# A fused Mamba and mixture-of-experts kernel on one core: the expert part moved to earlier slots, u and delta*u in one buffer

## The reference, cut to what matters

```python
x = x + layernorm(mamba(layernorm(x)))      # the first residual is called x1 here
x = x + layernorm(moe(layernorm(x)))

# mamba, D_INNER = 512, 16 states, 4 taps
x_in, z = split(x @ W_in)
u = silu(conv(x_in) + conv_b)
dt, B, C = split(u @ W_xproj)
delta = softplus(dt @ W_dt + b_dt)
h[t] = exp(delta[t] * A) * h[t-1] + (delta[t] * u[t]) * B[t]     # for each of 16 states n
y[t] = sum over n of h[t] * C[t] + D_skip * u[t]
out = (y * silu(z)) @ W_out

# moe: 2 shared and 8 routed experts of width 128
coef = top-2 of softmax(x @ router)
out = sum over e of (silu(x @ gate_e) * (x @ up_e)) @ down_e, times coef_e for the routed ones
```

## Time and profile before

| what | value |
|---|---|
| median of three runs | 2786.3 us |
| the profiled execution's own time | 2785.2 us |
| its span in the profile | 2783.4 us |
| first scan | 70.81 us |
| one body in the middle (scan of slot 0 to the next) | 166.50 us |
| end of the last scans to the end of the span | about 100 us |

### The profile page before, as it was taken

How to read it: one execution, slowest core, us unless ns; L and a number is a source line. 1 busy time by engine, 2 the same in 40 slices (tenths; PEclk the granted TensorE clock), 3 DMA queues, 4 the chain that set the end, 5 groups by cost and what they waited for, 6 DMA issues and landing times. The chain is left out here.

```text
span 2783.4 us, 31976 instructions
## 1 busy us (share of the span) xinstructions
PE 2355.8 (85%) x9920; PEld 1493.7 (54%) x9920; DVE 2325.4 (84%) x3308; ACT 1844.2 (66%) x2632; POOL 1789.7 (64%) x1470
## 2 busy tenths in 40 slices
PE   6678988889798888988889798898988889797878
PEld 3345655556455555655556455555655556455554
DVE  2899888888889888888888889888888888889970
ACT  3555857768586685857768576685857768586652
POOL 2465775847668485675847668485775847658653
PEclk9758989999898998989999898998989999899899
DMA  3101111111111111121112111111111112111111
GB/s 109 34 32 43 49 58 35 54 39 57 50 43 46 48 49 49 47 60 35 53 39 57 49 43 47 43 54 50 46 61 35 53 39 58 38 43 52 52 42 38
DMA packets 92954, 134.38 MB, mean 48 GB/s; under 512 B 12000, under 2 KB 42976, under 8 KB 92784
## 3 DMA queue, kind: packets, MB, share of 16 engines
q1 hardware_dynamic: 92784, 132.34, 16.2%
HBM read 123.13 MB, written 9.18 MB: 48 GB/s over the span
## 5 line engine op out<-in xcount | busy, mean ns | idle before, releaser
L760 DVE TENSOR_TENSOR_SCAN h<-d_a,carry,d_bu 128x512 f32<-128x512 f32 x1024 | 1306.1, 1276 | 118.5 <-ACT d_a L596 112.0
L1000 POOL TENSOR_TENSOR d_bu<-delta_u,b_rows 128x1024 f32<-128x1024 f32 x512 | 1199.3, 2358 | 4.4 <-issue 0.2
L596 ACT ACTIVATE d_a<-delta,a_neg 128x512 f32<-128x512 f32 x1024 | 701.9, 689 | 608.3 <-DVE h L760 602.3
L448 PE MATMUL ht<-ident,h 128*128 128x128 f32 x4096 | 677.7, 295 | 184.4 <-DVE y_t L777 156.0
L448 PEld LDWEIGHTS ht<-ident,h 128*128 128x128 f32 x4096 | 525.0, 151 | 570.8 <-issue 284.6
L777 DVE SCALAR_TENSOR_TENSOR y_t<-ht,c_t,y_t 128x512 f32<-128x512 f32 x896 | 658.8, 735 | 126.4 <-PE ht L448 125.2
L1042 POOL TENSOR_TENSOR hidden<-silu_gate,up 128x512 f32<-128x512 f32 x160 | 203.9, 1274 | 346.5 <-issue 284.9
L530 PE MATMUL dn<-w_down_sb,hidden 128*128 128x256 f32 x1280 | 331.3, 405 | 90.6 <-POOL hidden L1047 69.8
L503 PE MATMUL ring<-x_t,w_gate_sb 128*128 128x512 f32 x640 | 328.7, 639 | 19.8 <-ACT delta L716 16.7
L530 PEld LDWEIGHTS dn<-w_down_sb,hidden 128*128 128x128 f32 x1280 | 247.0, 203 | 132.3 <-POOL hidden L1047 73.7
L510 PE MATMUL ring<-x_t,w_up_sb 128*128 128x512 f32 x640 | 303.8, 597 | 0.0
(11 more groups left out here) (114 smaller groups left out, 2410.3 us busy)
## 6 DMA issues: line engine op xcount, KB each, us to landing
b_rows<-b_rows_hbm SPq DMA_DIRECT2D x256, 256.0 KB, 3.5
coef_rows<-coef_rows_hbm SPq DMA_DIRECT2D x128, 256.0 KB, 3.5
xa<-L_attn_x_in SPq DMA_DIRECT2D x16, 512.0 KB, 5.0
xr<-L_attn_x_in SPq DMA_DIRECT2D x16, 512.0 KB, 3.8
out<-xr SPq DMA_DIRECT2D x16, 512.0 KB, 3.1
w_in_sb<-L_attn_W_in_in SPq DMA_DIRECT2D x1, 1024.0 KB, 6.4
w_gate_sb<-L_ffn_experts_gate_in SPq DMA_DIRECT2D x2, 512.0 KB, 5.0
w_up_sb<-L_ffn_experts_up_in SPq DMA_DIRECT2D x2, 512.0 KB, 5.7
```

Source lines behind the costliest of these rows:

```text
L448: last = nc.tensor.transpose(HT[q % HTS][:, j * P:(j + 1) * P], H[:, (NS * c + n) % HS, j, a * P:(a + 1) * P], IDN[:, :])
L596: nc.scalar.activation(DA[i % DAS][:, :], DL[:, r, j, :], ACT.Exp, scale=ANEG[:, j, n:n + 1]).then_inc(ex.sem, 1)
L760: nc.vector.tensor_tensor_scan(H[:, (NS * s + n) % HS, j, :], DA[(n * J + j) % DAS][:, :], BU[:, (2 * n + j // 2) % 4, j % 2, :], CARRY[:, ...
L1000: nc.gpsimd.tensor_tensor(BU[:, (2 * n + h) % 4, :, :], DU[:, 2 * h:2 * h + 2, :], BB[:, n % 2, :].unsqueeze(1).to_broadcast([P, 2, T]), A ...
```

## The change

The slots are set anew. The transposes, gates and output products of the former chunk stand closer together and earlier, the transposes of x1 go to the two `DN` banks and not through the ring, router and first gate product share slot 19, each expert keeps four slots, and its down product stands five slots behind its gate product, not six. So the last down product is in slot 60 of its own body, the moments of the result in slots 62 and 63, and its residual in slot 1 of the next. D_skip*u (`DU`) now comes before delta (`DL`). U has two buffers in turn, and delta*u is written over u, on GpSimd in slots 44, 45, 48 and 49. The core of the diff:

```diff
-        U = sb("u", [P, J, T])
+        U = sb("u", [P, 2, J, T])
         YD = sb("y_d", [P, J, T])
         SZ = sb("silu_z", [P, 2, NT, DI])
         DL = sb("delta", [P, 2, J, T])
-        DU = sb("delta_u", [P, J, T])
...
-        XIN_PE, TAP0_ACT = (2, 3, 9, 11), (3, 4, 10, 12)
-        TAP = ((4, 4, 4), (5, 5, 5), (11, 11, 12), (13, 13, 14))
-        YD_PE, YD_ACT, OUT_PE = (5, 6, 7, 8), (6, 7, 8, 9), 10
-        Z_PE = (13, 15, 18, 19)
-        SILU = {10: [("u", 0), ("u", 1)], 16: [("u", 2), ("u", 3), ("z", 0), ("z", 1)], 20: [("z", 2), ("z", 3)]}
-        XD_PE, X1T_PE, ROUTE_PE, GATE_PE, CT_PE, CF_PE = 17, 22, 24, 24, 27, 31
-        DL_PE, DL_ACT = (35, 35, 39, 39), (36, 36, 40, 40)
-        DU_PE, DU_ACT = (43, 43, 47, 47), (44, 44, 48, 48)
+        XIN_PE, TAP0_ACT = (5, 6, 9, 10), (6, 7, 10, 11)
+        TAP = ((7, 7, 8), (8, 9, 9), (11, 11, 11), (12, 12, 13))
+        YD_PE, YD_ACT, OUT_PE = (3, 3, 4, 4), (4, 4, 5, 5), 6
+        Z_PE = (12, 14, 17, 18)
+        SILU = {11: [("u", 0), ("u", 1)], 15: [("u", 2), ("u", 3), ("z", 0), ("z", 1)], 19: [("z", 2), ("z", 3)]}
+        X1T_PE, GATE_PE = 18, 19
+        XD_PE, CF_PE, CT_PE = 21, 25, 26
+        DU_PE, DU_ACT = (29, 30, 33, 34), (30, 31, 34, 35)
+        DL_PE, DL_ACT = (37, 37, 41, 41), (38, 38, 42, 42)
+        DU_POOL = (44, 45, 48, 49)
...
+        def silu_slot(f):
+            return GATE_PE + 4 * f + 1
...
-            return gate_slot(f) + 6
-
-        MIDDLE = {0: [("ct", 1, 0)], 1: [("cf", -1, 0)], 2: [("dl", 1, 0), ("dl", 1, 1)],
-                  3: [("dl", 1, 2), ("dl", 1, 3)], 4: [("du", 1, 0), ("du", 1, 1)],
-                  5: [("du", 1, 2), ("du", 1, 3)]}
-        RING_USE = [("xt", 1, 0, 0), ("xt", 1, 1, 1), ("xin", 1, 0, 0), ("xin", 1, 1, 1)]
+            return gate_slot(f) + 5
+
+        MIDDLE = {0: [("xd", 1, 0, 0)], 1: [("cf", -1, 0, 0), ("ct", 1, 0, 1)],
+                  2: [("du", 1, 0, 0), ("du", 1, 1, 1)], 3: [("du", 1, 2, 0), ("du", 1, 3, 1)],
+                  4: [("dl", 1, 0, 0), ("dl", 1, 1, 1)], 5: [("dl", 1, 2, 0), ("dl", 1, 3, 1)]}
+        RING_USE = [("xt", 1, 0, 0), ("xt", 1, 1, 1)]
         RING_USE += [("yd", -1, j, j % 2) for j in range(J)]
-        RING_USE += [("xin", 1, 2, 0), ("xin", 1, 3, 1), ("z", 1, 0, 0), ("z", 1, 1, 1), ("xd", 1, 0, 0),
-                     ("z", 1, 2, 1), ("z", 1, 3, 0), ("x1t", -1, 0, 0), ("x1t", -1, 1, 1)]
-        experts = [use for k in range(F) for use in [("gt", -1, k), ("up", -1, k)] + MIDDLE.get(k, [])]
-        RING_USE += [(*use, i % 2) for i, use in enumerate(experts)]
-
-        ring_free = {"yd": (yd, 1), "xt": (xt, 1), "xin": (conv, TAPS), "z": (sz, 1), "x1t": (x1t, 1),
+        RING_USE += [("xin", 1, j, j % 2) for j in range(J)] + [("z", 1, a, a % 2) for a in range(NT)]
+        for k in range(F):
+            RING_USE += [("gt", -1, k, 0), ("up", -1, k, 1)] + MIDDLE.get(k, [])
...
-                    if exists(lo - 2) and t == 10:
+                    if exists(lo - 2) and t == 3:
...
-                    if ffn and t == 12:
+                    if ffn and t == 4:
...
-                    if ffn and t < NT:
-                        transpose_state(s - 1, t - NT + SLOTS)
-                    if exists(lo - 2) and t == 1:
-                        down_part(s - 2, F - 1)
...
-                    if ffn and t in (20, 21, 23, 26):
-                        if t == 20:
-                            pe.wait_ge(resid["o"].sem, resid["o"].at(s - 1))
-                        keep_warm(DN[1])
+                    if ffn and t == 2:
+                        pe.wait_ge(*ring_user_before(s, lo, "yd", 0))
+                        keep_warm(ring_bank("yd", 0))
+                        keep_warm(ring_bank("yd", 0))
                     if ffn and t == OUT_PE - 1:
                         pe.wait_ge(resid["y"].sem, resid["y"].at(s - 2, 2))
                         keep_warm(DN[0])
                         keep_warm(DN[0])
+                    if ffn and t in (15, 16):
+                        if t == 15:
+                            pe.wait_ge(resid["o"].sem, resid["o"].at(s - 1))
+                        keep_warm(DN[1])
...
-                        pe.wait_ge(*ring_user_before(s, lo, "x1t", k))
-                        bank = ring_bank("x1t", k)
                         for a in range(NT):
-                            last = nc.tensor.transpose(bank[:, a * P:(a + 1) * P],
+                            last = nc.tensor.transpose(DN[k][:, a * P:(a + 1) * P],
...
-                if t == ROUTE_PE:
+                if t == GATE_PE:
...
-                    if exists(lo - 2) and t == 9:
+                    if exists(lo - 2) and t == 2:
...
-                        act.wait_ge(full["xd"].sem, full["xd"].at(c - 1))
-                        act.wait_ge(full["du"].sem, full["du"].at(c - 1))
-                        act.wait_ge(du.sem, du.at(c - 1))
-                        nc.scalar.activation(U[:, j, TAPS - 1:], ring_bank("xin", j)[:, TAPS - 1:], ACT.Identity,
+                        act.wait_ge(bu.sem, bu.at(c - 2))
...
-                    if ffn and t <= NT:
-                        add_state(s - 1, o, SLOTS + t - NT - 1)
-                        if t > 0:
-                            gate_y(s - 1, o, t - 1)
+                    if ffn and t == 0:
+                        add_state(s - 1, o, SLOTS - NT - 1)
+                    if ffn and t in (1, 2):
+                        for a in (2 * t - 2, 2 * t - 1):
+                            add_state(s - 1, o, SLOTS - NT + a)
+                            gate_y(s - 1, o, a)
...
-                if t in (3, 4):
-                    dve.wait_ge(down.sem, down.at(c))
-                    for a in (2 * t - 6, 2 * t - 5):
-                        moments("y", c, a, dn(a))
-                if t == 4:
-                    moments_end("y", c)
-                if t in (7, 8):
-                    for a in (2 * t - 14, 2 * t - 13):
+                if t == 1:
+                    for a in range(NT):
...
-                if t in (OUT_PE + 2, OUT_PE + 5):
-                    a = 0 if t == OUT_PE + 2 else 2
+                if t in (8, 11):
+                    a = 0 if t == 8 else 2
...
-                if t in (17, 18):
-                    for a in (2 * t - 34, 2 * t - 33):
+                if t in (13, 14):
+                    for a in (2 * t - 26, 2 * t - 25):
                         add_stream_o(c, a)
-                if t == 19:
+                if t == 15:
...
-                if t == ROUTE_PE + 1:
+                if t == GATE_PE + 1:
                     route(c, 0)
                     route(c, 1)
-                if ROUTE_PE + 3 <= t < ROUTE_PE + 7:
-                    for i in range(4):
-                        route(c, 4 * (t - ROUTE_PE - 3) + 2 + i)
-            def conv_part(c, t):
+                if t in (GATE_PE + 3, GATE_PE + 4):
+                    for i in range(8):
+                        route(c, 8 * (t - GATE_PE - 3) + 2 + i)
+                if t in (62, 63):
+                    dve.wait_ge(down.sem, down.at(c))
+                    for a in (2 * t - 124, 2 * t - 123):
+                        moments("y", c, a, dn(a))
+                    if t == 63:
+                        moments_end("y", c)
...
-                    if exists(lo - 2) and t == 5:
-                        rstd_of("y", s - 2)
-                    if ffn and t == OUT_PE + 5:
+                    if ffn and t == 63:
+                        rstd_of("y", s - 1)
+                    if ffn and t == 11:
                         rstd_of("o", s - 1)
-                    if ffn and t == 20:
+                    if ffn and t == 16:
...
+                for j in range(J):
+                    if t == DU_POOL[j]:
+                        pool.wait_ge(softplus.sem, softplus.at(c, j + 1))
+                        pool.wait_ge(full["xd"].sem, full["xd"].at(c))
+                        pool.wait_ge(full["du"].sem, full["du"].at(c))
+                        nc.gpsimd.tensor_tensor(U[:, o, j, :], DL[:, o, j, :], U[:, o, j, :], ALU.mult)\
+                          .then_inc(du.sem, 1)
...
-                    for j in (t - 60, t - 59):
-                        pool.wait_ge(softplus.sem, softplus.at(c, j + 1))
-                        pool.wait_ge(u_s.sem, u_s.at(c))
-                        if j == 0:
-                            pool.wait_ge(bu.sem, bu.at(s))
-                        nc.gpsimd.tensor_tensor(DU[:, j, :], DL[:, o, j, :], U[:, j, :], ALU.mult)\
-                          .then_inc(du.sem, 1)
```

More of the change, by code:

```diff
@@ L358, in body @@
                           .then_inc(xr_ld.sem, 16)
-                    if ffn and t in (33, 34):
-                        coef_row(s - 1, 1 - r, t - 33)
-                    if ffn and t > 34 and t % 4 == 1 and 2 <= (t - 29) // 4 < E:
-                        coef_row(s - 1, 1 - r, (t - 29) // 4)
-                    if prep and t == 22:
+                    if ffn and t in (CF_PE + 2, CF_PE + 3):
```

(31 more changed lines are left out.)

9 lines of the change are left out of this document (6 added, 3 removed).

## The result

The changed kernel takes 2855.6 us (2852.95 to 2856.72) where the kernel before takes 2786.7 beside it: a ratio of 1.025 [1.0237, 1.0262], slower by 69 us. The profiled execution has a span of 2854.6 us, 71.2 more than before. VectorE works 9 us less in total than in the earlier trace rows and waits more.

The account below looks back on a forecast made before the run. What can change is VectorE's waiting, about 20 us a chunk, since neither TensorE nor VectorE is simply the limit. Fourteen chunks at +5.0 (+70) and the tail (+16) give 86 on 2785.2, taken as 2872; range 2765 to 2925.

Parts of the forecast that it names:

- Slots 0 to 12, 42.1: Front of the chunk: two new VectorE waits, 5.7 us, replace 3.5 and a tap moves in; 38.94 becomes 42.1, +3.2.
- Slots 12 to 28, 44.4: Stretch with all routing: VectorE's waits 5.1 against 7.4, including 3.4 for the router; 46.86 becomes 44.4, -2.5.
- Slots 28 to 44, 35.9: Stretch that loses the routing operations, -2.7, its other waits at about the same price; 39.05 becomes 35.9, -3.15.
- Slots 44 to 64, 17.85 and 31.25: Deciding term: GpSimd late for the eighth expert's down product, VectorE waits 6.1; 16.90 becomes 17.85, 24.75 becomes 31.25.
- The sum, +5.0 for each of fourteen chunks: The stretches add up to 171.5 us a chunk, +5.0; fourteen chunks have all three parts: +70.
- Lead-in and body 0 at nothing: Lead-in within 1 us, y_init before delta with the same products; first chunk, without experts, nothing, -3 to +3.
- Body 15 at nothing: The chunk without preparation, so no delta*u on GpSimd: no change, -3 to +3 us.
- The tail, +16: Last chunk's experts: each from the second on takes 7.05 us, not 5.16; seven times 1.9 plus 2.9 at the start.
- Edits at nothing: Two u buffers, delta*u in place, earlier result store, moved b_store and coef_row, two more warmers a chunk: no cost.
- A: Rival, slots 0 to 5: low clock lengthens the queue to the second output product by 4 us, 2928 total; chance 0.14.
- B: Rival: one of two TensorE waits (GpSimd's 6.1 or the front's 5.7) is absorbed, tail stays, 2785 to 2815; chance 0.22.
- C: Rival: neither TensorE wait reaches VectorE, -6.8 us a chunk, faster kernel at 2706; chance 0.18.

Follow-up runs that it names:

- n1: The changed kernel with every expert's down product six slots behind its gate, as before, instead of five: 2786.8 us, 1.0003 of the kernel before.
- k4: The changed kernel with three warming products ahead of the eighth expert's down product, where TensorE waits for hidden: 2840.9 us, 1.0202 of the kernel before.
- k3: The changed kernel with the down product six slots behind its gate in the last chunk's experts alone: 2831.5 us, 1.017 of the kernel before.
- n5: The changed kernel without the two warming products of slot 5, ahead of the output products: 2825.5 us, 1.0146 of the kernel before.
- k1: The changed kernel with distance six, delta*u four slots earlier, first moments of o in slot 9, routing one slot later, no slot-5 warmers: 2717.3 us, 0.9753 of before.
- m1: The changed kernel with down products six slots behind the gate and delta*u in slots 40, 41, 44, 45: 2785.0 us, 1.0 of the kernel before.

## Why the prediction was right, step by step

**The kernel is slower because TensorE waits for GpSimd, at the eighth expert's down product and in the tail: right.** The forecast was 2872 and the time is 2855.6. n1 gives the whole loss back.

**The total is better than its parts.** The chunks came out 15 us below their sum, the lead-in and body 0 10.5 below; body 15 and the tail came out 4.2 and 6.2 above. These last 10.4 are cancelled by the 10.5 of the lead-in and body 0, and that is luck.

**Slots 0 to 12, 42.1: measured 41.59.** The taps of the first x_in wait 1.77 for 1.5, the moments of o 4.12 for 4.2.

**Slots 12 to 28, 44.4: measured 43.85.** The router's wait is 3.51 for 3.4, the Exp's 0.6 for 0.9.

**Slots 28 to 44, 35.9: measured 36.77.** One of the two stretches that came out longer than forecast, by 0.9. Here the waits were taken to keep their price; they rose from 5.4 to 6.6, all but 0.3 of them for transposes. For these first three stretches the changes named in the prediction add up to about +3.0, -2.3 and -2.7, a little off the +3.2, -2.5 and -3.15 that it takes; measured are +2.65, -3.0 and -2.3.

**Slots 44 to 64, 17.85 and 31.25: measured 18.81 and 29.65.** The place, the queue and the item were right, the size was not: VectorE waits 4.5, not 6.1, and TensorE 2.7, not 4.2. Two steps of the sum failed. The hidden of the seventh expert ended 0.3 us before slot 48 and not 0.6 after it, so the eighth's ended 11.3 after S48 and not 12.4. And TensorE came to the down product not at 140.85 but at 141.9, behind the transpose of slot 52 (the row at 1366.62), after slots 44 to 52 had taken 1.0 longer than forecast. The clock was 0.67 over the 5.25 us, not 0.5 throughout. The decay of slot 59 cost 0.9 for 1.0. The Trainium skill, "TensorE: Matmul & The Clock Gate", Part 1, puts the slow clock behind missing activity; the trace agrees (2.93 for 1.99 after a wait of 2.70, 1.99 again in k4 with products in the gap), but only about 1 us a chunk of the 2.2 that I gave it reached VectorE. That the chunk still came out within 0.8 is in part luck: slots 52 to 64 were 1.6 shorter than forecast, slots 28 to 52 1.8 longer.

**The sum, +5.0 for each of fourteen chunks.** The chunk after was 0.8 below the forecast. The chunk of 166.50 that stands in the earlier trace rows was one of the shortest in the middle, where the bodies run in a cycle of 166.5, 167.1 and 168.2: from 368.99 to 2375.37 are twelve bodies of 167.20 on average. That one-chunk sample took another 0.7 from the difference: 3.7 each, 44.2 for twelve. Body 14 was counted as one of the fourteen and has no difference: it prepares no rstd of x for GpSimd. Body 1 was worth 10.9, not 5. Of that the distance is 4.2 (n1); the other 6.7 weren't foreseen. 1.7 of them are VectorE's work, which rose from 141.5 to 143.2 there, since the moments of the result now stand in the chunk's own body. Together 55 for 70.

**Lead-in and body 0 at nothing: wrong, -10.5.** In body 0 VectorE's waits for the taps fell from 6.0 to 0.3 us and those for transposes from 5.3 to 2.8, which covers its 7.4. Whether the order of y_init and delta or the early x_in does it was not told apart. The 3.1 of the lead-in are not firm: in the versions above that don't touch it, the first scan comes anywhere from 66.9 to 70.1. **Body 15 at nothing: +4.2.** Its cause stays open. It isn't firm either: k3, which differs only behind it, has +1.8.

**The tail, +16: measured +22.** 7.13 an expert for 7.05 was right. Most of what was left out is the last interval: from the second to the tenth down product are eight, not seven. The last took 3.59 before and takes 7.13 now, 3.5 us more. The rest is the slow clock: the last down product runs 3.68 for 1.99 behind a wait of 3.42, 1.7 more. The first runs 2.81 behind a wait of 2.47, but with it the start costs 3.25, near the 2.9 forecast.

**Edits at nothing.** n1 has all of them, and bodies 2 to 13 cost 0.06 us each more than before, so together with the front they come to nothing. No run takes them one by one.

**Rivals.** A (low clock in front, 2928): half of it happens. The low clock is there in slots 1 to 4, and the two warmers of slot 2 run at it, but from slot 5 on the products run at full clock. The stretch from 1228 to 1236, columns as above, has a granted 0.50:

```profile
1228.00:1236.00 8.00, 6.30 (x21) 4.30 (x20) 7.90 (x13) 3.85 (x8) 4.68 (x8) 0.50 0.24 68
```

The four products of the warmers in slot 2 take 3.62 us (at 1233.78), those in slot 5 take 1.88 (at 1244.76). From there to the start of slot 12 the granted clock is 1.00. So the queue to the second output product did not grow by the 4 us that A needs. Over slots 0 to 12 the clock is 0.88, up from 0.78 in the earlier trace rows. The warmers of slot 5 are not what brings it back, since without them (n5) those products run at full clock too. Whether the warmers of slot 2 are was not tried. B and C fall with the rows at 1253.58 and 1375.83: the output product's wait is there whole (4.12 for 4.2), the other in large part (4.50 for 6.1). C's other half, that the kernel is faster with both waits away, is what k1 shows, with the routing moved as well: 2717 where C said 2706.

## What to carry to other kernels

In a hand-placed schedule of in-order queues, the distance between two items on one engine must cover the place where the other engine is latest, not its mean. One slot less between gate and down product was free at nine of ten experts of a chunk. In bodies 2 to 13 it cost 43 us at the one where GpSimd's queue was full, and 21 in the tail, where nothing else fills the distance. Before a step is moved closer, walk the producer's whole queue to its end. Take a chunk's time as the mean over a full cycle of chunks. A removed wait is worth what the next one behind it leaves: here 8.5 us in all for 3.5 a chunk.

## What the runs showed of the hardware that was not expected

The slow clock came behind shorter waits than the one of 4.85 us in the earlier trace rows: after 2.70 us (granted 0.67 over the next 5.25) and after 2.47 us in the tail (a down product of 2.81). It also came behind two waits of which neither is that long, 2.26 us and, four transposes later, 0.58. The tenth expert's down product in the same chunk of the kernel after:

```profile
1388.30 3.48 PE L536 MATMUL dn<-w_down_sb,hidden 128*128 128x256 f32 x8 [0.58 <-POOL hidden L1055]
```

In n1 the same product runs 3.04 behind waits of 1.76 and 1.11, and there VectorE waits 1.1 us for it. A wait of 1.71, seven times in a row in the tail at a period of 7.13, cost nothing (1.99 each time), nor did one of 1.64 in body 14.

Three warming products in the gap brought full clock (k4), and two ahead of the output products did nothing but delay them by their own 1.72 us (n5).

A higher clock on average does not mean a shorter time. Ten executions of m1 were granted 0.907 to 0.908 in five cases and 0.938 to 0.940 in the other five; the first took 2783.4 to 2784.8 us, the others 2785.3 to 2787.3.
